# First layer of a four-layer network as one list over 64 states, on one core

## What is computed

```python
xn = _layernorm(x)
x_part, z = jnp.split(xn @ in_proj_w.T + in_proj_b, 2, axis=-1)
x_conv = silu(conv4(x_part) + conv_b)
dt = softplus(x_conv @ dt_w.T + dt_b)
Bm, Cm = x_conv @ B_w.T + B_b, x_conv @ C_w.T + C_b
# per token t: h = exp(dt * A) * h + dt * Bm * x_conv ; y = sum_s h * Cm + D * x_conv
s = (y * silu(z)) @ out_w.T + out_b
g = silu(sum over the 2 chosen of 8 experts of weight * (gelu(xn @ w1 + b1) @ w2 + b2))
x = x + s * g
```

## Time and profile before

| | us |
|---|---|
| median of three runs | 2161.23 (2155.55 to 2161.79) |
| the profiled execution | 2168.38 |
| its span, first to last instruction | 2166.3 |
| mean granted TensorE clock in it | 0.805 of full speed |
| TensorE busy in the span | 1581.7 |
| VectorE busy | 1241.6 |
| ScalarE busy | 1064.4 |
| GpSimd busy | 223.0 |

### The profile page before, as it was taken

One profiled execution on the slowest core, in us unless ns is written; L12 is line 12 of the kernel. 1 busy time (PEld: TensorE's weight loads), 2 busy tenths in 40 slices (PEclk: granted clock), 3 DMA queues, 4 the chain that ended last, 5 costly groups with the idle time before them and its releaser, 6 DMA issues.

```text
span 2166.3 us, 24477 instructions
## 1 busy us (share of the span) xinstructions
PE 1581.7 (73%) x8520; PEld 788.8 (36%) x8520; DVE 1241.6 (57%) x2578; ACT 1064.4 (49%) x1590; POOL 223.0 (10%) x210
## 2 busy tenths in 40 slices
PE   5767667657758979789786677767677578786876
PEld 2443444434524544445443222322222322222442
DVE  4986968949856474664754423224222777673522
ACT  3955946928603323132234766666575022332575
POOL 0430422403300000000000000000000000000003
PEclk9987978879869999999998857667566567876899
DMA  6000000000031001010032311203010121021002
GB/s 251 1 1 0 0 1 0 0 0 0 0 93 38 23 2 52 8 46 15 2 94 110 103 30 41 62 20 98 15 51 22 32 72 53 29 56 53 1 2 64
DMA packets 71567, 83.39 MB, mean 38 GB/s; under 512 B 8864, under 2 KB 68256, under 8 KB 70816
## 3 DMA queue, kind: packets, MB, share of 16 engines
q1 hardware_dynamic: 69760, 77.28, 11.9%
q0 software_dynamic: 1696, 4.72, 0.8%
HBM read 50.77 MB, written 31.20 MB: 38 GB/s over the span
## 4 chain that ended last, share of the span: by engine, by line
PE 44%; DVE 25%; ACT 14%; issue 13%; DMA 2%; SPq 1%; POOL 1%; DVEq 0%; ACTq 0%; POOLq 0%
PE ps L1090 8%; PE ps L828 6%; PE ps L816 5%; DVE neg_max L1787 4%; PE ps L815 4%; ACT scratch L1361 3%; DVE mixture_sum L1533 3%; ACT ps L1343 2%; PE ps L1003 2%; PE ps L955 2%; DVE scratch L1639 2%; DVE gated L1507 2%; DVE hidden L1511 2%; DVE scratch L1628 1%; ACT tanh L1242 1%
## 5 line engine op out<-in xcount | busy, mean ns | idle before, releaser
L1361 ACT ACTIVATE scratch<-ps 128x1024 f32<-128x1024 f32 x272 | 274.4, 1021 | 238.4 <-PE ps L1060 63.2
L1787 DVE TENSOR_REDUCE neg_max<-ps 128x2 f32<-128x1024 f32 (+2 forms) x224 | 232.4, 1068 | 111.0 <-PE ps L1003 109.9
L1090 PE MATMUL ps<-scratch,values 128*32 128x512 f32 (+3 forms) x1280 | 190.3, 681 | 11.2 <-ACT scratch L1361 5.7
L1975 POOL TENSOR_TENSOR scratch<-scratch 128x512 f32<-128x512 f32 x128 | 160.3, 1273 | 361.3 <-DVE scratch L1639 361.3
L1242 ACT ACTIVATE tanh<-ps 128x512 f32<-128x512 f32 x88 | 52.6, 597 | 291.8 <-PE ps L816 291.8
L828 PEld LDWEIGHTS ps<-weights_even,hidden 128*128 128x128 f32 (+1 forms) x960 | 148.6, 227 | 96.7 <-issue 53.2
L828 PE MATMUL ps<-weights_even,hidden 128*128 128x128 f32 (+1 forms) x960 | 156.7, 316 | 34.7 <-DVE mixture_sum L1533 34.7
L1343 ACT ACTIVATE ps<-ps 128x512 f32<-128x512 f32 x256 | 150.8, 589 | 58.4 <-PE ps L1049 58.4
L1634 DVE TENSOR_TENSOR_SCAN scratch<-scratch 128x512 f32<-128x512 f32 x128 | 175.8, 1413 | 1.5 <-ACT scratch L1302 1.5
L816 PE MATMUL ps<-xnt_sequence,weights_even 128*128 128x512 f32 x256 | 151.4, 682 | 0.0
L1507 DVE SCALAR_TENSOR_TENSOR gated<-tanh,ps 128x512 f32<-128x512 f32 x88 | 60.4, 686 | 157.4 <-ACT tanh L1242 157.3
(11 more groups left out here) (286 smaller groups left out, 2724.0 us busy)
## 6 DMA issues: line engine op xcount, KB each, us to landing
scratch<-parts_scratch SPq DMA_DIRECT2D x288, 96.0 KB, 2.3
parts_scratch<-weights_even SPq DMA_DIRECT2D x168, 128.0 KB, 2.4
weights_odd<-in_l SPq DMA_DIRECT2D x1, 4224.0 KB, 28.1
weights_even<-in_l SPq DMA_DIRECT2D x1, 4096.0 KB, 17.2
weights_odd<-in_l SPq DMA_DIRECT2D x1, 4096.0 KB, 13.4
parts_scratch<-gated SPq DMA_DIRECT2D x15, 128.0 KB, 2.4
slots_scratch<-gated SPq DMA_DIRECT2D x5, 256.0 KB, 27.4
weights_even<-slots_scratch POOLq DMA_DIRECT2D x1, 1280.0 KB, 10.3
```

The lines of the kernel that those rows point to most:

```text
L1090: mm = pe.matmul(ps[32 * i:32 * i + 32, PV, q0:q0 + n], lhs, buf[:, slot, col:col + n], start=first_, stop=True, skip_group_check=True)
L1361: act.activation(dst, src, ACT.Exp).then_inc(q[l, "exp_done"], 1)
L1787: ins = dve.tensor_reduce(dst, ps[:, base:base + 2, col:col + n], AX.X, ALU.max, negate=True)
L1975: pool.tensor_tensor(l0["y"][:, g, :], l0["y"][:, g, :], l0["hc"][:, g, :], ALU.add)\
```

## The change

The loop over sequences goes. The first layer becomes a list of its own, `first_layer`, in front of the list of the other layers, over 64 states (`STATES`). An item names a piece of work and every engine does its part of it:

```diff
+STATES = NB * NST
+RING = 4
+HIDDEN = 8
+EXPERTS = NB * E0
...
+HEAD0_AT = {0: (("hx", 0),), 1: (("hx", 1),), 2: (("ht", 0),), 3: (("hx", 2), ("cv", 1)), 4: (("hx", 3), ("cv", 2)),
+            5: (("hz", 0), ("cv", 3)), 6: (("hv", 0),), 7: (("gate", 0), ("zs", 0)), 8: (("ge", 0), ("xv", 0)),
+            9: (("dt", 0), ("cw", 0)), 10: (("dt", 1), ("mb0", 0)), 11: (("br", 0), ("mb1", 0)), 12: (("hl", 0),),
+            13: (("ds", 0), ("y0", 0))}
+TAIL0_AT = {1: ("yg",), 2: ("op",), 3: ("cb",), 5: ("nm",), 6: ("tr",)}
...
+    for b in range(NB):
+        for s in range(NST):
+            n = NST * b + s
+            out.append(("s", 0, b, n))
+            if s % 2 == 0 and n + 2 < STATES:
+                out.append(("da", 0, (n + 2) // NST, n + 2))
+            if b:
+                out += [(what, 0, b - 1, 0) for what in TAIL0_AT.get(s, ())]
+            if b + 1 < NB:
+                out += [(what, 0, b + 1, k) for what, k in HEAD0_AT.get(s, ())]
+            m = n // 2 + 2
+            if s % 2 == 0 and m < EXPERTS:
+                out.append(("f", 0, m // E0, m))
```

VectorE keeps scans and C products of a state, with all operands in SBUF; GpSimd makes the input for the state after, with one 128x1024 instruction, and adds with another. Scanned states, products and inputs have buffers of their own (`hs` one, `hc` and `ub` two, `da` and the rows four):

```diff
+            def state(n):
+                dve.wait_ge(q[0, "u_ready"], n + 1)
+                for g in range(2):
+                    dve.wait_ge(q[0, "da_ready"], 2 * n + g + 1)
+                    if n:
+                        dve.wait_ge(q[0, "hc_ready"], 2 * (n - 1) + g + 1)
+                    dve.tensor_tensor_scan(hs[:, g, :], da[n % RING][:, g, :], ub[n % 2][:, g, :], 0.0, ALU.mult, ALU.add)\
+                       .then_inc(q[0, "scan_done"], 1)
+                if n >= 2:
+                    dve.wait_ge(q[0, "state_added"], n - 1)
+                for g in range(2):
+                    dve.wait_ge(q[0, "scan_done"], 2 * n + g + 1)
+                    tt(hc[n % 2][:, g, :], hs[:, g, :], bc_rows[n % RING][:, 1, :], ALU.mult).then_inc(q[0, "hc_ready"], 1)
...
+            def driven(n):
+                b = n // NST
+                pool.wait_ge(rows_in[n % RING], 16 * (n // RING + 1))
+                if n >= 2:
+                    pool.wait_ge(q[0, "scan_done"], 2 * (n - 1))
+                pool.wait_ge(q[0, "dt_ready"], b + 1)
+                row = bc_rows[n % RING][:, 0:1, :].to_broadcast([P, 2, T])
+                pool.tensor_tensor(ub[n % 2][:, :, :], sets[b % 2]["dtx"][:, :, :], row, ALU.mult)\
+                    .then_inc(q[0, "u_ready"], 1)
...
+                if what == "s":
+                    if n == 0:
+                        driven(0)
+                    if n + 1 < STATES:
+                        driven(n + 1)
+                    if n:
+                        added(n - 1)
```

B and C rows no longer go through the selector products, which are removed with `sel` and the splitting of the rows. ScalarE takes the 32 rows from PSUM, SP writes them to memory and fetches, for each state, its two rows onto all partitions. Layer 1's weights follow in ninths during the last sequence, the zeros for `slots_scratch` during the first, and layer 2's weights behind layer 1's first stacks:

```diff
+            def states(b):
+
+                sp.wait_ge(q[0, "head_seen"], 7 * b + 7)
+                sp.dma_start(bc_d[b % 2], bcf).then_inc(q[0, "rows_out"], 16)
+                sp.wait_ge(q[0, "rows_out"], 16 * (b + 1))
+                for s in range(NST):
+                    n = NST * b + s
+                    if n >= RING:
+                        sp.wait_ge(q[0, "hc_ready"], 2 * (n - RING + 1))
+                    pair = bc_d[b % 2].rearrange("(k s) t -> s k t", k=2)[s:s + 1]
+                    sp.dma_start(bc_rows[n % RING][:, :, :], pair.to_broadcast([P, 2, T])).then_inc(rows_in[n % RING], 16)
```

More of the change, by code:

```diff
@@ L175, in constants @@
     slope = 0.5 ** np.arange(NH)
-    sel = np.zeros((P, 2 * NST, P), f)
-    for s in range(2 * NST):
-        sel[[s, 2 * NST + s, 4 * NST + s], s] = 1
     c16 = blob([
@@ L466, in flow @@
         if not l:
+            out += first_layer(head_items(1, 0))
             continue
@@ L470, in flow @@
             continue
-        if l == 1:
-            out += head_items(l, 0)
         for b in range(NB):
@@ new lines, in later_tap @@
+            def later_tap(b, k):
+                dve.wait_ge(q[0, "head_seen"], 7 * b + 2)
+                for g in range(2):
+                    if k == 1:
+                        dve.wait_ge(q[0, "tap_ready"], 2 * b + g + 1)
+                    else:
+                        dve.wait_ge(q[0, "conv_ready"], 6 * b + 2 * (k - 2) + g + 1)
+                    stt(xc[:, g, :], xp[:, g, k:k + T], small[:, KC * g + k:KC * g + k + 1], xc[:, g, :],
+                        ALU.mult, ALU.add).then_inc(q[0, "conv_ready"], 1)
@@ new lines, in added @@
+            def added(n):
+                b = n // NST
+                y = sets[b % 2]["y"]
+                if n % NST == 0:
+                    pool.wait_ge(q[0, "y_begun"], 2 * (b + 1))
+                else:
+                    pool.wait_ge(q[0, "state_added"], n)
+                pool.wait_ge(q[0, "hc_ready"], 2 * n + 2)
+                pool.tensor_tensor(y[:, :, :], y[:, :, :], hc[n % 2][:, :, :], ALU.add).then_inc(q[0, "state_added"], 1)
+            own.wait()
+            for b in range(NB):
+                t = slice(TB * b, TB * (b + 1))
+                pool.wait_ge(var_ready["pre"], b + 1)
+                own.link(pool.tensor_scalar(vare0[:, t], mv0[:, t, 1], EPS, None, ALU.add))
+                pool.tensor_tensor(rstd0[:, t], vare0[:, t], half[:, :], ALU.pow).then_inc(rstd_ready["pre"], 1)
@@ new lines, in _ @@
+            pool.memset(ot[:, :], 0.0).then_inc(q[3, "zeros_ready"], 1)
+            for what, l, b, n in steps:
+                if what == "s":
+                    if n == 0:
+                        driven(0)
+                    if n + 1 < STATES:
+                        driven(n + 1)
+                    if n:
+                        added(n - 1)
+                elif what == "yg" and b == NB - 1:
+                    added(STATES - 1)
+                elif what == "cb":
+                    serve(0, b + 1, "straight")
```

734 lines of the change are left out of this document (387 added, 347 removed).

## The result

| | before | after |
|---|---|---|
| median, us | 2161.5 of 4 (2155.6 to 2162.9) | 2205.2 of 4 (2198.8 to 2210.1) |
| profiled execution | 2168.4 | 2198.8 |
| first scan | 58.8 | 75.5 |
| states: from there to the end of the last C product | 526.4 (from 57.17 on) | 573.5 |
| from there to layer 1's first scores | 40.2 | 18.4 |

The changed kernel takes 1.022 times as long (95% interval 1.0184 to 1.0257), 43.7 us more, where I had forecast 18. The first layer accounts for it: its end, read as layer 1's first scores, is 43.6 us later. That the two figures agree to 0.1 us is chance: the two profiled executions differ by 30.7 us.

A forecast was written before the change was run, and what follows sets the result against it. VectorE alone was taken to bound the first layer's states at 5.46 us each, with half-idle stretches between sequences. Terms -177 + 175 + 45 + 5 - 14 - 16 = +18 us gave a median of 2179, range 2090 to 2250.

The forecast's parts named there:

- Point 6: Kernel start: with less loaded and normalised first, the projection starts near 10 us; -14 us, ends 0 and -20.
- Points 2 and 3: First layer: states at 8.2 us in place of 5.46, +175; heads and tails among the states, +45 and +5.
- Point 1: Stretches without states between sequences go, as heads and tails spread over neighbours' states: -177 us.
- Point 4: ScalarE and TensorE in the first layer are no bound, even with head work added: nothing.
- Point 5: Rows of B and C come by transfer, 512 KB a state, hidden by four buffers; layer 1's weights hidden too.
- Point 7: End of the first layer: experts done, layer 1's q and k among the last states; -16 us, ends -6 and -25.
- A: Rival: C products and heads are not held by GpSimd, only scans are; 2054 to 2100 us, chance 0.15.
- B: Rival: nothing is held any more, ScalarE's own work bounds the first layer; 1968 us, chance 0.03.
- point 2: States: VectorE and GpSimd take turns, 8.2 us a state, +175 us; mixture steps covered by GpSimd, otherwise 35 us.
- C: Rival: four changes of engine a state cost 0.2 us each, +51 us; 2230 us, chance 0.15.
- D: Rival: row transfers come late, at 10 us each the states wait, +115 us; 2294 us, chance 0.05.

The follow-up runs named there:

- e14: Changed kernel with mixture steps two states later, TensorE's constants wait only ahead of layer 1, gate search behind the taps: 2165.7 us, 1.0026 of the kernel before.
- e12: Changed kernel with only the experts' mixture steps moved two states later in VectorE's list: 2176.7 us (one run).
- e7: Changed kernel without GpSimd's input products and additions, so VectorE has the states for itself: 2027.5 us (one run).
- e9: Changed kernel with input products on VectorE, scan inputs and states in two PSUM banks taken from the experts: 2203.9 us, 1.0175 of the kernel before.
- e4: Changed kernel with C products reading a fixed PSUM tile, not the C row, and one bank for the experts' downs: 2153.5 us (one run).
- e10: e9 with mixture steps two states later and two banks each for ups and downs: 2111.8 us, 0.9774 of the kernel before.
- e11: e10 with TensorE's constants wait only ahead of layer 1 and the gate search behind the taps: 2102.1 us, 0.9734 of the kernel before.
- e13: e11 with GpSimd's addition also waiting for the next state's input product: 2036.7 us, 0.9438 of the kernel before.

## Why the prediction was wrong

Direction right, size not: 43.7 us for 18. By its points:

- **Point 6, the start, is the step that failed.** It said -14 us (ends 0 and -20), the first scan near 45. The scan came at 75.5, 16.7 us later than before and not 14 sooner. I had looked at what is loaded and normalised first, and not at the order in which VectorE's list names the work: the first mixture step ahead of state 0, the gate search ahead of the taps, TensorE's wait for constants queued behind the experts' weights. The order of the list was there to be read. e14 has the first scan at 49.6 with these three put right, so the start that I forecast was nearly to be had, in another list.
- **Points 2 and 3, right in mechanism and, by luck, in sum.** 64 x 8.2 + 50 = 575 forecast, 573.5 measured. But e12 and e14 show 557 without the circle of experts and scans, 18 us under the sum, so a state costs nearer to my lower end of 7.9 than to 8.2. The other 16 us were VectorE's waits for downs among the states (39.3 us of them after the first scan, GpSimd working on in part of the time). I had booked the mixture steps at nothing, as covered by GpSimd. Of the 37 us that they last, only some 19 lay beside a GpSimd instruction in the kernel after (28 of 36 in e12; added up from the timelines), and their wait was not asked about. These are misses of opposite sign. With the start, too, put right (e14) the first scores came 1.9 us later than before, so for the lists that I had in mind +18 was too much.
- **Point 1** (-177) is not seen apart from these: the sum of 1 to 3 came out at +47.0 for +48. **Point 4:** ScalarE was busy 279 us and TensorE 309 in 573, no bound as busy times, but their chain of ups, gelus and downs is what bounded the start and, in e7 and e9, held up the states (72 and 116 us of waits at the mixture steps among them). "Nothing" was wrong for the chain, right for the engines.
- **Point 5, the rows,** held; the ninths of layer 1's weights are 519.5 KB each, where I had 532. Transfers of the kernel after (issues, KB, us to landing):

```profile
scratch<-state_rows SPq DMA_DIRECT2D x64, 512.0 KB, 4.8
...
weights_odd<-in_l SPq DMA_DIRECT2D x8, 519.5 KB, 6.4
```
GpSimd waited 1.9 us for rows in the whole kernel.
- **Point 7** gave -21.8 for -16, within its ends.

Laid end to end the table gives the whole: the states begin 18.3 us later (75.5 for 57.2), last 47.0 longer (573.45 for 526.43), and what follows is 21.8 shorter (18.4 for 40.2): +43.6 (by the unrounded times), where the forecast had -14 + 48 - 16 = +18. Of the difference of 25.6 us the start makes 32.3 too many, the tail gave 5.8 more than forecast and the states 1.0.

The rivals: A (products not held) is out, since products with both inputs in SBUF are held up to 2.85 us beside GpSimd, and those with one input in PSUM (e4, e9) are not; B is out with it (its sum had the mixture steps at 43 us where point 2 had 35, but ScalarE bounded it anyway); C, costs of handing over, would have made states of over 8.2 us, and they are under it; D is out by the transfers. The Trainium skill ("SBUF — State Buffer", section "SBUF: two separate sides") states that a VectorE instruction with two SBUF inputs and a GpSimd instruction that reads SBUF hold the shared ports by turns, whichever starts first. The traces agree: held with two SBUF inputs (2849 ns for a product of 658), not with one of them in PSUM (682 at worst, e4), not with GpSimd idle (691, e7), and GpSimd held as well as VectorE (4343 ns for 2340). The estimate of 2.35 us for 1024 elements, worked out in the forecast from this case's 1273 ns and the 4497 ns for 2048 elements of the Trainium skill ("GPSIMD Engine Reference", section "Performance versus the Vector engine"), agrees with the additions' 2330 ns at least and 2359 in the middle.

## What to carry to other kernels

When an engine's program is a list, read at the start, and where the lists meet, what stands ahead of the awaited instruction and whom that waits for: 32 steps of 1.1 us each cost 29 us in all by their place. Work that shuts another engine out is priced by the sum of both, so give it to the engine that needs less of the shared time, keep one operand in PSUM where a bank is free, and place the rest beside instructions that don't exclude it; here that, with the lists put right, turned 2% slower into 5.6% faster. Read an experiment that takes a bound away together with its waits: e9 freed every scan and gained 4.5 us, because the next bound, the experts' chain, stood right behind and had lost two banks to it.

## What was not expected of the hardware

- The input product reads two SBUF tensors and writes PSUM, and is held all the same (2853 ns for 681, e10): where it writes does not matter, where it reads does. e10's expectation had allowed some 25 us for it; holding the addition back gave 68. A scan with its decay in SBUF, its input in PSUM and its result in the same PSUM bank is never held (1.224 us at worst, e9) and costs the same as one in SBUF.
- The same 150 us of GpSimd additions cost 68 us of states or not, by a shift of some 1.3 us in when each starts (e11, e13).
- A 512 KB transfer in which all partitions read the same 4 KB took 4.8 us, less than the 6.4 of one of 519.5 KB of weights with different bytes for each.
